# Gating a chunk after the scans of state 4 instead of state 2 in VectorE's order of a Mamba layer

## The reference, cut to what matters

```
xh, z = split(x @ W_in);  xh = silu(conv2(xh))
dt_low, Bmat, Cmat = split(xh @ W_x);  dt = softplus(dt_low @ W_dt + b_dt)
dA = exp(dt * A);  dBx = dt * B * xh          # per step, 256 channels x 16 states
h = dA * h + dBx                              # the scan over the sequence
y = sum over states of h * C,  + xh * D
y = y * silu(z)                               # the gate
out = y @ W_out
```

## Time and profile before

| what | value |
|---|---|
| time, median of 3 runs | 16281.83 us (16277.56 to 16301.75) |
| time of the profiled execution | 16276.23 us |
| span of the profiled execution | 16274.4 us |
| VectorE busy | 13974.3 us (86%) |
| TensorE busy | 14161.2 us (87%) |
| GpSimd busy | 13069.0 us (80%) |
| ScalarE busy | 10107.5 us (62%) |
| mean granted TensorE clock | 0.925 |

### The profile page before, as it was taken

How to read it: one execution, slowest core, us unless ns; L and a number is a source line. 1 busy time by engine, 2 the same in 40 slices (tenths; PEclk the granted TensorE clock), 3 DMA queues, 4 the chain that set the end, 5 groups by cost and what they waited for, 6 DMA issues and landing times. The chain is left out here.

```text
span 16274.4 us, 144588 instructions
## 1 busy us (share of the span) xinstructions
PE 14161.2 (87%) x40704; PEld 5407.5 (33%) x40704; DVE 13974.3 (86%) x13537; ACT 10107.5 (62%) x14054; POOL 13069.0 (80%) x5647
## 2 busy tenths in 40 slices
PE   8999997888888888888888888888888888888886
PEld 3333332333333333333333333333333333333332
DVE  1222228999999999999999999999999999999997
ACT  2222225666666666666666666666666676666675
POOL 0000007999999999999999999999999999999996
PEclk9999998999999999999999999999999999999997
DMA  1111104444445545444455454454544444545544
GB/s 50 42 39 44 39 26 151 171 161 169 170 172 180 180 168 180 173 178 171 175 182 181 168 180 173 176 182 164 182 178 172 177 176 175 182 167 181 180 173 172
DMA packets 560359, 2505.37 MB, mean 154 GB/s; under 512 B 58695, under 2 KB 171063, under 8 KB 293448
## 3 DMA queue, kind: packets, MB, share of 16 engines
q1 hardware_dynamic: 549272, 2477.68, 42.9%
q10 hardware_dynamic: 10288, 18.44, 0.4%
HBM read 2325.32 MB, written 170.57 MB: 153 GB/s over the span
## 5 line engine op out<-in xcount | busy, mean ns | idle before, releaser
L794 POOL TENSOR_TENSOR hc<-h,c_all 128x1024 f32<-128x1024 f32 x4096 | 9531.7, 2359 | 574.0 <-DVE h L1161 496.1
L1031 PE MATMUL y_ps<-hc,ident 128*128 128x512 f32 x16392 | 8392.7, 664 | 1127.8 <-POOL hc L794 1127.6
L892 ACT ACTIVATE d_a<-dt,a_neg 128x512 f32<-128x512 f32 x8194 | 5596.1, 689 | 4081.4 <-DVE h L1161 4055.4
L1161 DVE TENSOR_TENSOR_SCAN h<-d_a,h,dbx_v 128x512 f32<-128x512 f32 x5456 | 6622.0, 1262 | 10.4 <-DVE dbx_v L1148 1.1
L1031 PEld LDWEIGHTS y_ps<-hc,ident 128*128 128x128 f32 x16392 | 3362.3, 211 | 6055.1 <-issue 4172.5
L1148 DVE TENSOR_TENSOR dbx_v<-dtx_ps,b_all 128x1024 f32<-128x1024 f32 x2816 | 3313.7, 1206 | 61.0 <-issue 26.2
L1161 DVE TENSOR_TENSOR_SCAN h<-d_a,h,dbx_p 128x512 f32<-128x512 f32 x2480 | 3027.7, 1262 | 10.8 <-issue 0.4
L783 POOL TENSOR_TENSOR dbx_p<-dtx,b_all 128x1024 f32<-128x1024 f32 x1280 | 3002.3, 2355 | 23.8 <-DVE h L1161 0.8
L480 POOL MEMSET ident_f<- 128x128 f32 x1 | 0.2, 205 | 2417.5 <-POOLq L45 2417.5
L273 PE MATMUL conv_ps<-image,w_taps 128*32 128x512 f32 x11520 | 1777.7, 594 | 0.0
L363 DVE RECIPROCAL k_inv<-k_nrm 128x4 f32<-128x4 f32 x256 | 45.5, 178 | 1774.2 <-ACT k_nrm L215 1774.2
(11 more groups left out here) (143 smaller groups left out, 9228.5 us busy)
## 6 DMA issues: line engine op xcount, KB each, us to landing
b_all<-bc_dram SPq DMA_DIRECT2D x1028, 1024.0 KB, 6.3
c_all<-bc_dram SPq DMA_DIRECT2D x1025, 1024.0 KB, 5.0
o_dram<-o_sb SPq DMA_DIRECT2D x257, 256.0 KB, 6.2
o_c<-o_dram SPq DMA_DIRECT2D x220, 256.0 KB
out<-r_c SPq DMA_DIRECT2D x220, 256.0 KB, 7.9
image<-in_x SPq DMA_DIRECT2D x91, 512.0 KB, 4.1
un<-un_dram SPq DMA_DIRECT2D x736, 34.0 KB
bc_dram<-low_bc SPq DMA_DIRECT2D x257, 64.0 KB, 4.6
```

What stands on the lines that cost most here:

```text
L794: nc.gpsimd.tensor_tensor(hc[:, n % HC], h[:, n], c_all[:, n // CG % 2, n % CG].unsqueeze(1).broadcast_to([128, 2, CH]), ALU.mult).then_in ...
L892: nc.scalar.activation(d_a[:, half], dt[:, p, half], ACT.Exp, scale=a_neg[:, half, n:n + 1]).then_inc(a_done, 1)
L1031: last = nc.tensor.matmul(y_ps[:, half], ident[:], hc[:, n % HC, half], start=False, stop=(n == S - 1))
L1161: nc.vector.tensor_tensor_scan(h[:, n, half], d_a[:, half], dbx, zero_col[:] if first else h[:, n, half, CH - 1:CH], ALU.mult, ALU.add).th ...
```

## The change

In VectorE's order for a chunk, the gate of the previous chunk moves from behind the scans of state 2 to behind the scans of state 4. The product `weigh(km, 4)` and the four scans of states 3 and 4, which stood behind it, now stand ahead of it. Nothing else is changed; no instruction is added or removed.

```
                 weigh(km, 3)
                 run_scan(km, 2, 0, first)
                 run_scan(km, 2, 1, first)
-                gate(km, q)
                 weigh(km, 4)
                 run_scan(km, 3, 0, first)
                 run_scan(km, 3, 1, first)
                 run_scan(km, 4, 0, first)
                 run_scan(km, 4, 1, first)
+                gate(km, q)
                 weigh(km, 5)
                 weigh(km, 6)
                 run_scan(km, 5, 0, first)
```

## The result

The changed kernel takes 17317.6 us (median, 17312.6 to 17324.1) against 16286.0 us (16277.6 to 16301.8) for the kernel before: ratio 1.063, interval 1.061 to 1.065. It is 1032 us slower, where 17,520 us were forecast with a range from 17,100 to 17,770. The profiled execution took 17312.6 us with a span of 17310.7 us.

The account below looks back on a forecast made before the run. VectorE bounds, idle almost only at the gate: 16,118 us without its reachable waits, plus 1339 us (248 chunks at 2.4 + 3.0 us) and 19 and 38 us at images' last chunks: 17,514, say 17,520 us; range 17,100 to 17,770.

Parts of the forecast that it names:

- What bounds: VectorE bounds phase B, idle almost only at the gate, 167.7 us; the change removes all but the last gate's 10.0 us.
- The six last chunks: At six images' last chunks scan 3 waits for its decay, queued behind silu_x on ScalarE: 6 x 6.4 = 38 us.
- silu_z: ScalarE's silu_z waits for the gate but can start no later than now: no cost.
- The path over low: Gate, add_skip, three added states, project_x, low, decays of state 7: VectorE idles 2.4 us a chunk ahead of scan 7.
- The clock: TensorE's new idle stretch ahead of add_skip brings the low clock, lengthening the path to low by 3.0 us a chunk.
- the two bounds of 1.70 and 3.04 us: Low clock's extra time for eight TensorE matmuls behind 4.3 us of idle time; the forecast took the upper, 3.0 us.
- GpSimd: hc of state 4 waits for add_state(0): up to 2.5 us a chunk, hidden by scan 7's loss; as bound, chance 0.03.
- Only reordered: VectorE's work up to scan 7 is only reordered, so it still wants scan 7 at 9026.10.
- The sum: 5.4 us a chunk over 248 chunks, 1339 us, plus 19 and 38 us on 16,118: 17,514, say 17,520 us.
- The rule of the Trainium skill: Find the most contended engine's gaps and start their enders sooner; taken alone it would book 158 us at the gate.

Follow-up runs that it names:

- a1_fill: Changed kernel with four extra full-size TensorE matmuls per chunk in the idle stretch between gated and add_skip: 16929 us, ratio 1.040.
- a2: Changed kernel with project_x moved ahead of add_state(1) and add_state(2) in TensorE's order: 16747 us, ratio to before 1.029.
- a3: Changed kernel with ScalarE's low moved behind the decays of states 7 and 8: 16734 us, ratio to before 1.028.
- b1: Kernel before with the gate moved by one product only, behind weigh(km, 4), 1.13 us later: 16222 us, ratio 0.996.
- c1: b1 with a third buffer for VectorE's products dbx_v, small tensors sharing memory to make room: 16156 us, ratio to before 0.992.
- b2: Kernel before with the gate moved behind the scans of state 3, 3.5 us later: 16720 us, ratio 1.027.
- b6: b2 with two extra full-size TensorE matmuls ahead of gated: 16378 us, ratio to before 1.006.
- a6_both: Changed kernel with the edits of a2 and a3 together: 16763 us, ratio to before 1.030.

## Why the prediction was right, point by point

- **What bounds**, right: VectorE, with the gate as its one idle place. The waits of 158 us that the change can reach are gone.
- **The six last chunks**, right: 38 us were forecast ahead of scan 3 behind silu_x, and ScalarE's decay holds VectorE up for 41.9 us.
- **silu_z**, right: it costs nothing at this place of the gate.
- **The path over low**, right in each link. Its start was 0.31 us too late: I took the 0.36 us between gate and add_skip from the earlier trace rows, but there add_skip waited for gated as well; it starts 0.05 us behind the gate. The clock-free price was put at 2.4 us and is 2.0 us (a1_fill).
- **The clock**, right as a mechanism and too large as a term: 3.0 us forecast, 9.33 - 7.13 = 2.2 us measured. It lies between the two bounds of 1.70 and 3.04 us, whose mean (2.4) would have been the better choice. The argument for the upper end failed on its own step: I said that the stretch would grow to 7 us, as states 14 and 15 would be added earlier against the gate. It stayed at 5.6 us on the mean. GpSimd's product of state 11 waits for scan 7 (the 528.6 us of L783 above), which ties GpSimd, and TensorE's states with it, to the later VectorE.
- **GpSimd**, right as far as the traces tell: hidden behind the stall at scan 7, and what is left once that is gone, 2.3 us a chunk over the 52.34 us of an undisturbed one (a2 and a3 take 54.6 us in the median chunk) against at most 2.5 us forecast.
- **Missed**: the 0.24 us ahead of `weigh(km, 4)`, 61 us in all (35 us of idle time, the rest lost overlap). "Only reordered" was not free: the gate had stood between a scan and the product that reuses its buffer.
- **The sum**: 16,118 for what remains, 1086 of idle time ahead of scan 7, 42 ahead of scan 3, 35 ahead of `weigh(km, 4)` and 37 us more of VectorE's busy time (14011.6 against 13974.3) make 17,318, against 17,313 measured. The busy time grows since two operations that wait no longer overlap with the one before them: 0.08 us at scan 7 and at `weigh(km, 4)` in each chunk are 41 us. The forecast's 1339 + 19 = 1358 us for the path was 272 too high, of which 248 x 0.8 = 198 is the clock and 248 x 0.31 = 77 the start; the missed terms gave 72 back. So 17,520 came within 202 us by a path that was right and a clock term that was over a third too large.

The rule of the Trainium skill that the forecast weighed (Perfetto Trace Analysis, section Optimization Strategy: find the gaps of the most contended engine and make what ends them start sooner) would have booked 158 us for this change; taken with the question who waits for the gate, b1 shows it at work, 64 us, and c1 66 us more for a gap ahead of a product.

## What to carry to other kernels

Before an operation is moved back in a saturated engine's order, follow what waits for it through the other engines' fixed orders until the chain comes back to the saturated one, and add up its cover: here 3.2 us at full clock, against a move of 5.85 us. The low clock behind the new idle stretch took 2.2 us of that cover, and beyond it every microsecond of the move was a microsecond of each chunk. Moving a wait out of reach by the smallest step that covers it (b1) gained; moving it further lost. And an operation that stands between two dependent ones on the same engine hides their latency, so that what takes its place should be looked at too.

## What the runs showed of the hardware that was not expected

- The low clock behind an idle stretch of TensorE was about as costly at 3.24 us of idle time (b2, 9.34 us for a burst of 7.13) as at 5.64 (changed kernel, 9.33). Shorter stretches did not rule it out: at 1.3 and 2.3 us (b6, a1) 103 and 99 of 256 chunks still met it, and in b1, at 0.57 us, 92, with 8.8 to 8.9 us for the burst. In the three kernels before, b1 and b2, whose TensorE does the same work, the slow bursts are 8, 92 and 250 of 256. What decides below 3 us, no run shows.
- A dependence between two neighbouring operations of VectorE cost 0.24 us here (scan, then the product that reuses its buffer), and a third buffer took 66 us off the kernel.
- a1_fill, a2_x_first, a3_low_later, a6_both and b2_gate_s3, five different edits, all have a median chunk of 54.61 to 54.63 us, although their means differ (55.0 to 55.8). The kernel before has 52.34 and 53.4 us in turn. In the traces of a2 and b2 the granted clock falls at the same two places of most chunks (0.8 and 14.5 us behind the first product in b2), while in the kernel before the places change from chunk to chunk. That this is what sets the common length was not tried.
